# The adapter's layers on float32r halves instead of f32, with four banks for the up tiles

## What is computed

```python
h  = x * ((cond @ norm_w.T + 1.0)[:, None, :] * rsqrt(mean(x * x) + 1e-6))
val, gate = split(h @ up_w.T)                 # up_w: 4096 x 512
h  = val * gelu(gate)
x1 = act_quant(h) @ weight_quant(down_w).T + x

Wd_b = Wd + 0.1 * (cond @ Wdd.T + bdd)        # 128 x 512 for each batch
Wu_b = Wu + 0.1 * (cond @ Wdu.T + bdu)        # 512 x 128 for each batch
down = relu(x1 @ Wd_b.T + bd)
out  = x1 + down @ Wu_b.T + bu
```

## Time and profile before

| | us |
|---|---|
| median of three runs | 979.3 (978.88 to 979.54) |
| the profiled execution | 978.98 |
| its span in the trace | 976.8 |
| TensorE busy / share of the span | 962.9 / 99% |
| VectorE busy | 654.7 |
| ScalarE busy | 444.5 |
| GpSimd busy | 52.2 |
| mean granted TensorE clock | 0.998 |

### The profile page before, as it was taken

The page is one execution under the profiler, slowest core; times in us unless marked ns, Lnnn a source line. Parts: engine busy times, 40 slices in busy tenths (PEclk is TensorE's granted clock), DMA queues, the critical chain, the costliest instruction groups (busy, mean ns, idle before and its releaser), DMA issues.

```text
span 976.8 us, 13713 instructions
## 1 busy us (share of the span) xinstructions
PE 962.9 (99%) x5344; PEld 468.5 (48%) x5344; DVE 654.7 (67%) x1032; ACT 444.5 (46%) x819; POOL 52.2 (5%) x52
## 2 busy tenths in 40 slices
PE   7999999999999999999999999999999999999998
PEld 5555544444444444444444444444444444445453
DVE  6878887656876687756876587657776584236333
ACT  4888656323751267224651267214741265117122
POOL 1000000000000000000000000000000000000554
PEclk9999999999999999999999999999999999999999
DMA  9434543544344443544434443444344432210674
GB/s 331 143 130 145 200 130 98 161 142 128 114 132 144 130 130 103 157 140 140 119 130 129 137 133 117 132 142 139 119 141 123 147 130 69 83 54 22 223 246 177
DMA packets 73305, 134.59 MB, mean 138 GB/s; under 512 B 5268, under 2 KB 10904, under 8 KB 72728
## 3 DMA queue, kind: packets, MB, share of 16 engines
q1 hardware_dynamic: 73240, 133.72, 43.0%
HBM read 112.72 MB, written 20.97 MB: 137 GB/s over the span
## 4 chain that ended last, share of the span: by engine, by line
PE 97%; DVE 1%; DMA 0%; issue 0%; ACT 0%; SPq 0%; DVEq 0%
PE bank L918 23%; PE bank L920 23%; PE bank L919 23%; PE bank L971 10%; PE bank L930 6%; PE bank L1092 3%; PE bank L1105 3%; PE bank L981 1%; PE bank L891 1%; PE bank L901 1%; PE bank L1083 1%; DMA xn<-in_x 0%; PE bank L955 0%; PE bank L961 0%; PE bank L910 0%
## 5 line engine op out<-in xcount | busy, mean ns | idle before, releaser
L918 PE MATMUL bank<-x_split,w_hi 128*128 128x512 f16 x1024 | 389.1, 380 | 2.3 <-DVE x_split L654 2.3
L919 PE MATMUL bank<-x_split,w_hi 128*128 128x512 f16 x1024 | 388.7, 380 | 0.0
L920 PE MATMUL bank<-x_split,w_lo 128*128 128x512 f16 x1024 | 388.6, 379 | 0.0
L691 DVE STREAM_TRANSPOSE delta_reg<-delta_reg 128x512 f32<-128x512 f32 x256 | 261.6, 1113 | 12.8 <-PE bank L930 12.8
L529 ACT ACTIVATE g<-h 128x512 f32<-128x512 f32 x128 | 80.6, 630 | 263.9 <-DVE h L764 263.9
L764 DVE SCALAR_TENSOR_TENSOR h<-bank,desc,g 128x512 f32<-128x512 f32 x128 | 94.7, 740 | 114.5 <-issue 90.4
L518 ACT ACTIVATE g<-bank,desc 128x512 f32<-128x512 f32 x128 | 87.6, 684 | 170.4 <-PE bank L920 170.3
L918 PEld LDWEIGHTS bank<-x_split,w_hi 128*128 128x128 f16 x1024 | 100.3, 98 | 127.0 <-issue 10.5
L920 PEld LDWEIGHTS bank<-x_split,w_lo 128*128 128x128 f16 x1024 | 100.4, 98 | 121.4 <-issue 0.8
L919 PEld LDWEIGHTS bank<-x_split,w_hi 128*128 128x128 f16 x1024 | 100.4, 98 | 111.8 <-issue 0.6
L971 PE MATMUL bank<-wqT,qreg 128*128 128x512 bf16 x448 | 101.3, 379 | 0.0
(11 more groups left out here) (131 smaller groups left out, 593.2 us busy)
## 6 DMA issues: line engine op xcount, KB each, us to landing
delta_reg<-in_L_cond_Wdd SPq DMA_DIRECT2D x64, 512.0 KB, 3.7
delta_reg<-in_L_cond_Wdu SPq DMA_DIRECT2D x64, 512.0 KB, 3.7
qreg<-in_L_cond_up_w SPq DMA_DIRECT2D x32, 256.0 KB, 4.2
xr<-in_x SPq DMA_DIRECT2D x30, 256.0 KB, 4.2
x_scratch<-xr SPq DMA_DIRECT2D x30, 256.0 KB, 4.6
xn<-in_x SPq DMA_DIRECT2D x7, 1024.0 KB, 6.8
out_y<-w_hi SPq DMA_DIRECT2D x7, 1024.0 KB, 4.9
h<-in_L_cond_down_w SPq DMA_DIRECT2D x4, 1024.0 KB, 7.6
```

Of the source, the lines that this page charges most:

```text
L691: last = dve.transpose(natT[:, t, kk, :, :].rearrange("p a (r e) -> p e a r", e=4), nat[:, u % NAT, kk, :])
L918: pe.matmul(bank[:, :], w_hi[:, k, cols], xh[:, par, k, :], start=(k == 0), stop=False)
L919: pe.matmul(bank[:, :], w_hi[:, k, cols], xl[:, par, k, :], start=False, stop=False)
L920: mm = pe.matmul(bank[:, :], w_lo[:, k, cols], xh[:, par, k, :], start=False, stop=(k == KD - 1))
```

## The change

The adapter's matmuls take operands of type float32r. Each f32 operand is written as a high half (the value rounded to float32r) and a low half (the value less the high half), and each product becomes three: high x high, high x low, low x high. VectorE makes the low halves of the weights (from a scratch, s_bc), of x1 and of the down layer's output; ScalarE writes the high half of x1 and takes the relu twice, once to float32r and once to f32. The down layer writes into the bank that also holds x1's first transposes (x1_bank[0]), so x1 is turned in the order 1, 2, 3, 0. The up layer has a bank for each of its four tiles, with the high products of all four tiles first and then the low ones. In the hand-over, the transposes and the down layer of chunk 1 go behind the quantised products, which now fill the up tiles' banks; VectorE lowers x1 chunk 0 ahead of quantising. The tensors get buffers of their own in place of the views.

```diff
+        wd_lo = sb("wd_lo", [P, NB, D], F32R)
+        wu_lo = sb("wu_lo", [P, KD, NB, BN], F32R)
+        wd_hi = sb("wd_hi", [P, NB, D], F32R)
+        wu_hi = sb("wu_hi", [P, NB, D], F32R)
+        x1_hi = sb("x1_hi", [P, 2, KD, CH], F32R)
+        out_buf = sb("out_buf", [P, 2, TT, D], F32)
+        x1_lo = sb("x1_lo", [P, 2, KD, CH], F32R)
+        down_hi = sb("down_hi", [P, 2, CH], F32R)
+        down_lo = sb("down_lo", [P, 2, CH], F32R)
+        down_f32 = sb("down_f32", [P, 2, CH], F32)
...
-        up_bank = [HY, TB, Y, TB]
-        down_bank = [TA, HY] + [TA] * (NCH - 2)
+        up_bank = [HY, TB, Y, TA]
+        x1_order = (1, 2, 3, 0)
...
+            def copy_x1(c, par):
+                if c >= 2:
                     act.wait_ge(down_full, c - 1)
+                for i, k in enumerate(x1_order):
+                    act.wait_ge(x1_turned, KD * c + i + 1)
+                    act.activation(x1_hi[:, par, k, :], x1_bank[k][:, :], ACT.Copy).then_inc(x1T_done, 1)
 
             def relu_down(c, par):
                 act.wait_ge(down_full, c + 1)
+                if c >= 2:
                     act.wait_ge(up_full, TT * (c - 1))
-                act.activation(down_T[:, par, :], down_bank[c][:, :], ACT.Relu, bias=bdc[:, 0:1]).then_inc(relu_done, 1)
+                    act.wait_ge(down_split, c - 1)
+                for half in (down_hi, down_f32):
+                    act.activation(half[:, par, :], x1_bank[0][:, :], ACT.Relu, bias=bdc[:, 0:1]).then_inc(relu_done, 1)
...
             copy_x1(0, 0)
-            copy_x1(1, 1, (0, 1))
             copy_scales(NCH - 1)
-            copy_x1(1, 1, (2, 3))
             round_tiles(0, 1)
             relu_down(0, 0)
-            round_tiles(1, 4)
-            relu_down(1, 1)
-            round_tiles(4, FT // 2)
-            copy_x1(2, 0)
-
-            for c in range(2, NCH):
+            round_tiles(1, FT // 2)
+            copy_x1(1, 1)
+
+            for c in range(1, NCH):
                 relu_down(c, c % 2)
                 if c + 1 < NCH:
                     copy_x1(c + 1, (c + 1) % 2)
...
             def layer_of_batch(b):
+                for i, (turned, base_w, hi, lo) in enumerate((
+                        (HY[:, :], base_wd[:, :], wd_hi[:, b, :], wd_lo[:, b, :]),
+                        (TB[:, :], base_wu[:, :], wu_hi[:, b, :], wu_lo[:, :, b, :]))):
+                    dve.wait_ge(delta_turned, 2 * b + i + 1)
+                    if b + i > 0:
+                        dve.wait_ge(layers_split, 2 * b + i)
+                    dve.scalar_tensor_tensor(s_bc[:, :], turned, DELTA_SCALE, base_w, ALU.mult, ALU.add).then_inc(layers_ready, 1)
+                    dve.wait_ge(layers_ready, 2 * b + i + 1)
+                    dve.tensor_copy(hi, s_bc[:, :]).then_inc(layers_hi, 1)
+                    dve.wait_ge(layers_hi, 2 * b + i + 1)
+                    if i == 0:
+                        dve.tensor_tensor(lo, s_bc[:, :], hi, ALU.subtract).then_inc(layers_split, 1)
...
+            def x1_lower(c, par):
+                for i, k in enumerate(x1_order):
+                    dve.wait_ge(x1T_done, KD * c + i + 1)
+                    dve.tensor_tensor(x1_lo[:, par, k, :], x1_bank[k][:, :], x1_hi[:, par, k, :], ALU.subtract).then_inc(x1_split, 1)
+
+            def down_lower(c, par):
+                dve.wait_ge(relu_done, 2 * c + 2)
+                dve.tensor_tensor(down_lo[:, par, :], down_f32[:, par, :], down_hi[:, par, :], ALU.subtract).then_inc(down_split, 1)
...
             finish_max(NCH - 1)
+            x1_lower(0, 0)
             dve.wait_ge(s_bc_done, NCH)
-            for k in range(0, FT, 2):
+            quantise_last(0)
+            quantise_last(2)
+            down_lower(0, 0)
+            for k in range(4, FT, 2):
                 quantise_last(k)
...
+            for t in range(TT):
+                residual(NCH - 1, t, up_bank[t])
+            x1_lower(1, 1)
             add_up(0, 0)
...
+            for c in range(1, NCH):
+                down_lower(c, c % 2)
+                if c + 1 < NCH:
+                    x1_lower(c + 1, (c + 1) % 2)
                 add_up(c, c % 2)
...
+            def turn_x1(c, b, par):
+                pe.wait_ge(x1_in[par], 16 * (b + 1))
+                for i, k in enumerate(x1_order):
+                    if is_first(c):
+                        pe.wait_ge((gelu_done, h_done)[k % 2], FT * NCH - 1 + k // 2)
+                    elif k == 0:
+                        pe.wait_ge(relu_done, 2 * c)
                     else:
+                        pe.wait_ge(x1_split, KD * (c - 1) + i + 1)
...
             def down_layer(c, b, par):
+                pe.wait_ge(layers_split, 2 * b + 2)
+                pe.wait_ge(x1_split, KD * (c + 1))
                 for k in range(KD):
-                    mm = pe.matmul(down_bank[c][:, :], wd_all[:, b, k * BN:(k + 1) * BN], x1T[:, par, k, :], start=(k == 0), stop=(k == KD - 1))
+                    cols = slice(k * BN, (k + 1) * BN)
+                    pe.matmul(x1_bank[0][:, :], wd_hi[:, b, cols], x1_hi[:, par, k, :], start=(k == 0), stop=False)
+                    pe.matmul(x1_bank[0][:, :], wd_hi[:, b, cols], x1_lo[:, par, k, :], start=False, stop=False)
+                    mm = pe.matmul(x1_bank[0][:, :], wd_lo[:, b, cols], x1_hi[:, par, k, :], start=False, stop=(k == KD - 1))
                 mm.then_inc(down_full, 1)
 
             def up_layer(c, b, par):
-                pe.wait_ge(relu_done, c + 1)
+                pe.wait_ge(relu_done, 2 * c + 1)
                 for t in range(TT):
+                    rows = slice(t * P, (t + 1) * P)
+                    if is_first(c):
+                        pe.wait_ge(y_done, TT * (NCH - 1) + t + 1)
+                    else:
+                        pe.wait_ge(up_done, TT * (c - 1) + t + 1)
+                    pe.matmul(up_bank[t][:, :], down_hi[:, par, rows], wu_hi[:, b, :], start=True, stop=False)
+                    pe.matmul(up_bank[t][:, :], down_hi[:, par, rows], wu_lo[:, :, b, :], start=False, stop=False)
+                pe.wait_ge(down_split, c + 1)
+                for t in range(TT):
+                    rows = slice(t * P, (t + 1) * P)
+                    pe.matmul(up_bank[t][:, :], down_lo[:, par, rows], wu_hi[:, b, :], start=False, stop=True).then_inc(up_full, 1)
 
             turn_x1(0, 0, 0)
             turn_absrun(NCH - 1)
-            turn_x1(1, 0, 1, (0, 1))
             spread_scales(NCH - 1)
-            turn_x1(1, 0, 1, (2, 3))
             down_layer(0, 0, 0)
-            down_layer(1, 0, 1)
             last_down_products()
-            pe.wait_ge(relu_done, 2)
-            pe.wait_ge(s_bc_done, NCH)
-            pe.wait_ge(y_done, TT * (NCH - 1))
+            turn_x1(1, 0, 1)
             up_layer(0, 0, 0)
-            up_layer(1, 0, 1)
-            turn_x1(2, 1, 0)
-
-            for c in range(2, NCH):
+            for c in range(1, NCH):
                 down_layer(c, c // 2, c % 2)
```

More of the change, by code:

```diff
@@ L8 @@
 BF16 = mybir.dt.bfloat16
+F32R = mybir.dt.float32r
 I32 = mybir.dt.int32
@@ L52, in sem @@
             return ctx.enter_context(nc.semaphore(name))
[L55 to L58, removed]
         wqT = sb("wqT", [P, FT, D], BF16)
@@ L112, in conditioned_block @@
         bdc = sb("bdc", [P, 1], F32)
+        with (nc.sbuf_tensor("delta_reg", [P, NAT + NATT, 1024], F32) as delta_reg,
+              nc.sbuf_tensor("w_hi", [P, KD, 2 * FF], F16) as w_hi,
+              nc.sbuf_tensor("w_lo", [P, KD, 2 * FF], F16) as w_lo):
+            pass
+        wd_lo = sb("wd_lo", [P, NB, D], F32R)
[8 more added lines that the diff above has]
+        down_f32 = sb("down_f32", [P, 2, CH], F32)
+        nat = delta_reg[:, 0:NAT, :].rearrange("p s (k e) -> p s k e", k=2)
+        natT = delta_reg[:, NAT:, :].rearrange("p s (k a m) -> p s k a m", k=2, a=HB)
         bank = [ctx.enter_context(nc.psum_tensor(f"bank{i}", [P, 512], F32)) for i in range(8)]
@@ L181, in conditioned_block @@
             "nat_turned", "delta_mm", "stage_full", "stage_free"))
-        delta_back, delta_turned, layers_ready = (sem(n) for n in ("delta_back", "delta_turned", "layers_ready"))
+        delta_back, delta_turned, layers_ready, layers_hi, layers_split = (sem(n) for n in (
+            "delta_back", "delta_turned", "layers_ready", "layers_hi", "layers_split"))
         xr_in = [sem(f"xr_in{i}") for i in range(2)]
@@ L703, in layer_of_batch @@
             def layer_of_batch(b):
[L704 to L709, removed]
+                for i, (turned, base_w, hi, lo) in enumerate((
[11 more added lines that the diff above has]
+                    else:
+                        dve.tensor_tensor(lo, s_bc[:, :].rearrange("p (k n) -> p k n", k=KD),
+                                          hi.rearrange("p (k n) -> p k n", k=KD), ALU.subtract).then_inc(layers_split, 1)
+            def x1_lower(c, par):
[5 more added lines that the diff above has]
```

(5 more changed lines are left out.)

35 lines of the change are left out of this document (1 added, 34 removed).

## The result

The changed kernel takes 984.5 us (median; 984.05 to 985.96) against 979.4: the ratio is 1.0058, with a 95% interval of 1.0046 to 1.0071. It is slower by 5.2 us, where 4.3 us less was forecast: the sign was wrong, and the time lies at the very top of the range (985.0), which was drawn for other reasons: a dearer product and the weights and the clock at their worst. The profiled execution's span is 982.0 us (972.7 forecast, 976.8 before).

What follows compares the result with a forecast made beforehand. TensorE, busy 99% of the span, was taken as the bound. Quantised products end at 910.9, the last down layer at 964.6 (968.7 before), span 972.7 (4.1 less than 976.8); forecast 975.0 us, range 968.5 to 985.

Steps and rivals of the forecast that it cites:

- a dearer product: Adapter's float32r product: a price up to 0.29 us, allowed for in the range's upper end of 985.
- the clock: Hand-over: after idle time TensorE runs eight products at the 1.2 GHz level, 1.7 us lost (0 to 3.4).
- It frees GpSimd 5.27 us later: Adapter's loop: a store frees GpSimd 5.27 us after issue; bias adds of 4.95 us follow, then the next load.
- Rival 1: Loop: each load takes 8.0 us beside a store; time 978.3 us, no measurable change; no chance of its own given.
- Price of a product: Adapter: one float32r product takes 0.216 us, so an adapter product costs 0.648 us instead of 0.857.
- Rivals 2 and 3: Adapter's products: exposed weight load, 991.5 us (0.07), or half rate, 1011 us (0.09); run as f32, some 1090 us (0.03).
- Weights, last chunk: First layer's last chunk: added VectorE work delays TensorE's second turn 0.49 us for three batches; +1.5 us (0 to +2.4).
- Hand-over: Between first layer and loop: quantised products end at 910.9 against 910.25 before, so no gain so far.
- Chunk without a wait: Adapter's loop: TensorE's and VectorE's paths both give 7.2 to 7.3 us a chunk, against 8.81 before.
- Waits for loads: Loop, turns 4 to 7: TensorE waits for x1 loads held by a chain of transfers, some 3.9 us in all.

Runs made afterwards that it cites:

- the last run: Changed kernel with six output buffers, x1-store wait moved to load of chunk 7, small stores, then load 3, then store 0, weights' sums first, 15 fillers: 973.2 us, ratio 0.9942.
- all mendings together: Changed kernel with six output tiles, moved x1-store wait, small stores first, store of chunk 0 ahead of load 3, weights' sums first, fillers: 974.6 us, ratio 0.995.

## Why the prediction was wrong

The wrong step is one term of the loop: "It frees GpSimd 5.27 us later". That was the time of a store issued at 930.96, 0.7 us ahead of a load. The load's issue in the kernel before:

```profile
931.63 0.36 SPq L316 DMA_DIRECT2D x_split<-x_scratch  x1
```

There it was the load, second of the two, that paid, with 8.0 us; the prediction took this price for loads and none for a store that comes second. It had worked out that load 3 would go out at 917.9 and store 0 at 918.2, and put them down at 7.5 and 5.27 us. They went out at 918.82 and 919.24 and took 8.6 and 10.8 us. The 5.6 us that GpSimd started later behind the store's issue (10.9 instead of 5.3) are 5.6 us of the load behind it and of TensorE. The turn of chunk 4 came at 941.46 instead of 934.8; 1.0 of these 6.7 us is the store's later issue (919.24, forecast 918.2), the rest is this term. Rival 1 had the right mechanism and too small a size: it made the loads slow, and forgot that a store is slowed by a load.

Point by point, in the times of the forecast:

- *Price of a product*: 0.228 us, where 0.216 was taken. Rivals 2 and 3 are out. At 24 products that is 0.3 us a chunk. The weight load takes 0.20 us, like the f32 one of the earlier trace rows (0.19) and not like an f16 one (0.098). The Trainium skill (TensorE: Matmul & The Clock Gate, "Weight-path perf modes") says that the fast load is off for FP32 input; the record agrees for float32r, and that load is hidden all but for at most 0.012 us, the difference of 0.228 and 0.216. Whether that comes from the load was not tested.
- *Weights, last chunk*: 1.9 us lost, 1.5 forecast. The chain was as priced (cast 0.43, subtraction 0.69), with a gap of 0.1 instead of 0.04 at the second sum. The run with the sums first gave back all of it in this stretch, and 1.7 us of the whole.
- *Hand-over*: the clock fell as put, but 11 products ran slow, not 8, and the down layer took 5.2 us instead of 4.3. Quantised products began at 897.71 (897.1 forecast) and chunk 1's transposes at 911.76 (910.9). So weights and hand-over together lost 1.5 us against the earlier trace rows where 0.7 was said. The run with fillers shows the clock's part, 2.4 us.
- *Chunk without a wait*: 7.2 to 7.3 us said, 7.56 measured (950.39 to 957.95, and again in the last run). The price of 24 products is 0.3 of it; the relus hold the transposes up by 0.2 (they take 1.93 us from 950.39 and 1.72 behind the stop at 927.50), where 0.3 was said.
- *Waits for loads*: foreseen in kind for turns 4 to 7, 3.9 us in all. They were 6.5 us at turn 4 and none later, since that stop let all loads catch up; but the transposes behind it ran at the low clock, 1.6 us that no term had. Together that is turn 5 at 950.39 (942.1 forecast), 8.3 us late. From there the distance stays between 8.2 and 8.8 us up to the end of the last down layer and is 9.3 at the end of the span (982.0 less 972.7): the waits forecast for turns 5 to 7 did not come, and longer chunks took their place.
- *The second gate*, the wait for the x1 stores ahead of load 4, stood in the prediction nowhere. It cost nothing in the changed kernel, but it would have taken half of the gain from anyone who mended only the buffer.

Against the kernel before, then: the profiled execution of the changed kernel is 0.2 us ahead at the first turn of deltas, loses 1.9 by the weights and gains 0.2 in the rest up to 911.76, which makes the 1.5; turn 3 starts 2.8 us later (927.50 against 924.67), with chunk 1's transposes and down layer now in this stretch. From there to the end of down layer 7 the kernel before takes 44.0 us for five chunks and the changed one 45.9, of which 8.1 are the stop and the slow transposes: without them it would be 37.8, or 7.56 a chunk. The last 0.5 us of the 5.2 are lost behind the last down layer.

## What to carry to other kernels

When a loop gets shorter, list the transfers of each pass with their issue times, and price those that now go out within a microsecond of each other as a pair; a time read from a transfer that went out first is no price for one that goes out behind another. Give the head of the queue to the transfer that someone waits for. And a wait that costs nothing today may be the second gate behind the one you are about to open: follow the mended chain once more before counting the gain.

## What the runs showed of the hardware that I had not expected

A store of 1 MB issued 0.4 us behind a load of 1 MB on the same queue landed after 10.8 and 11.3 us; issued ahead of the load it landed after 7.8, and then the load took 9.8. In the kernel before, a load 0.7 us behind a store took 8.0. In all these pairs the one issued second paid more. The rate of the queue does not account for it alone. With the store ahead it was 399 to 407 GB/s from 919 to 925 us. In the changed kernel it was 219 to 287 there, which may hold part of the 10.8 us. With the small stores first and the load ahead it was 368, 266 and 390 from 921 to 927, and the store still took 11.3. How the transfers are served inside, and where the lower rate comes from, was not looked into.

After its stop of 6.5 us TensorE's granted clock was 0.50, and sixteen transposes took 3.3 us. After stops of 3.8 us (six output tiles alone) and 2.9 us (three product groups left out, its turn 6) the transposes were slow as well; after 1.7 us (all mendings together) they weren't. The expectation that a stop of 2 to 3 us would be too short for the clock to fall was never met by such a stop in its own run, and the one of 2.9 us speaks against it.
